# Fourth attention: the next x is turned ahead of the scores, and the query is projected between the turn of the outputs and the values

## The reference

```python
# _layernorm(x) is what comes in as modality1, ctx_768 as modality2
x1 = layernorm(modality1, ln1_g, ln1_b)      # so x is normalized twice
x2 = layernorm(modality2, ln2_g, ln2_b)
q = x1 @ Wq + bq
k = x2 @ Wk + bk
v = x2 @ Wv + bv
scores = jnp.einsum('bqe,bke->bqk', q, k) * scaling
attn = jax.nn.softmax(scores, axis=-1)
ctx = jnp.einsum('bqk,bke->bqe', attn, v)
return ctx @ Wo + bo
```

## Time and profile before

| | |
|---|---|
| median of three runs | 1800.82 us |
| time of the profiled execution | 1798.77 us |
| its span, first to last instruction | 1796.9 us |
| mean granted clock of TensorE | 0.950 |
| PE busy | 1619.2 us (90% of the span) |
| DVE busy | 981.3 us (55%) |
| ACT busy | 624.8 us (35%) |
| POOL busy | 333.5 us (19%) |
| fourth attention, first scores to last projection | 1490.6 to 1646 us |

### The profile page before, as it was taken

One profiled execution on the slowest core, in us unless ns is written; L12 is line 12 of the kernel. 1 busy time (PEld: TensorE's weight loads), 2 busy tenths in 40 slices (PEclk: granted clock), 3 DMA queues, 4 the chain that ended last, 5 costly groups with the idle time before them and its releaser, 6 DMA issues.

```text
span 1796.9 us, 31011 instructions
## 1 busy us (share of the span) xinstructions
PE 1619.2 (90%) x9150; PEld 1153.7 (64%) x9150; DVE 981.3 (55%) x3200; ACT 624.8 (35%) x1772; POOL 333.5 (19%) x465
## 2 busy tenths in 40 slices
PE   6898899859999999999999999799998998887787
PEld 2555555659999866666666667567776446665555
DVE  4778787542222244444444435645555666884764
ACT  3555555412323233333333333133332004552232
POOL 4555555320000130000000000100000122333000
PEclk8999999869999989999999989899998999998887
DMA  4000005248999610000000000100000001310000
GB/s 109 15 18 20 20 19 146 65 138 298 321 327 319 232 41 13 7 12 12 12 12 6 1 4 16 31 26 19 19 25 1 27 25 35 91 56 1 1 19 19
DMA packets 86297, 115.80 MB, mean 64 GB/s; under 512 B 16610, under 2 KB 77762, under 8 KB 81090
## 3 DMA queue, kind: packets, MB, share of 16 engines
q1 hardware_dynamic: 82722, 110.43, 19.1%
q0 software_dynamic: 2432, 4.34, 0.8%
q10 hardware_dynamic: 1056, 0.01, 0.0%
HBM read 104.51 MB, written 6.95 MB: 62 GB/s over the span
## 4 chain that ended last, share of the span: by engine, by line
PE 73%; issue 9%; DVE 7%; ACT 4%; DMA 2%; POOL 2%; ACTq 1%; SPq 0%; DVEq 0%; POOLq 0%
PE bank L2293 14%; PE bank L2406 8%; PE bank L2589 7%; PE bank L2379 5%; PE bank L2682 5%; PE bank L2352 5%; PE bank L2390 4%; PE bank L2436 4%; PE bank L2603 3%; PE bank L2344 3%; PE bank L2635 3%; PE bank L2651 3%; PE bank L2754 2%; DMA work<-in_F_b1c 2%; DVE work L1542 1%
## 5 line engine op out<-in xcount | busy, mean ns | idle before, releaser
L1052 ACT ACTIVATE work<-bank,work 100x361 f32<-100x361 f32 (+1 forms) x272 | 158.9, 591 | 253.5 <-DVE work L1542 231.6
L1551 DVE COPY work<-bank 128x300 f32<-128x300 f32 (+1 forms) x272 | 123.2, 490 | 175.6 <-PE bank L2390 174.9
L2406 PEld LDWEIGHTS bank<-work 128*100 128x100 f32 x1760 | 185.4, 171 | 45.5 <-issue 31.4
L2406 PE MATMUL bank<-work 128*100 128x64 f32 (+1 forms) x1760 | 188.2, 258 | 4.2 <-DVE work L1551 4.2
L2589 PE MATMUL bank<-work 128*128 128x128 f32 x1216 | 144.4, 277 | 3.7 <-DMA work<-in_F_b1c 3.7
L1905 DVE SCALAR_TENSOR_TENSOR work<-bank,work 128x128 f32<-128x128 f32 x160 | 56.1, 351 | 163.8 <-PE bank L2589 151.6
L2589 PEld LDWEIGHTS bank<-work 128*128 128x128 f32 x1216 | 142.0, 193 | 5.3 <-issue 3.5
L1542 DVE TENSOR_REDUCE work<-bank 100x1 f32<-100x361 f32 x208 | 101.8, 528 | 70.9 <-PE bank L2379 65.7
L823 POOL TENSOR_TENSOR work<-work,neg_half 100x1 f32<-100x1 f32 x96 | 52.5, 547 | 391.8 <-DVE work L1498 390.1
L2379 PE MATMUL bank<-work 64*100 64x361 f32 (+1 forms) x512 | 119.0, 542 | 1.1 <-ACT work L1037 0.6
L2293 PE MATMUL bank<-L_WkvT,work 96*128 96x512 f32 x192 | 98.2, 637 | 15.8 <-ACT work L1013 14.9
(11 more groups left out here) (306 smaller groups left out, 2907.9 us busy)
## 6 DMA issues: line engine op xcount, KB each, us to landing
work<-in_F_w SPq DMA_DIRECT2D x58, 1024.0 KB, 5.5
work<-in_ctxT SPq DMA_DIRECT2D x64, 135.4 KB, 2.1
work<-in_ctx SPq DMA_DIRECT2D x32, 192.0 KB, 2.5
work<-in_F_b SPq DMA_DIRECT2D x20, 128.0 KB, 5.8
work<-sorted_x SPq DMA_DIRECT2D x20, 128.0 KB, 2.5
sorted_y<-work SPq DMA_DIRECT2D x20, 128.0 KB, 5.3
work<-in_ctx SPq DMA_DIRECT2D x32, 78.8 KB, 2.4
F_weight<-in_F_w SPq DMA_DIRECT2D x2, 1024.0 KB
```

Source lines behind the costliest of these rows:

```text
L1052: nc.scalar.activation(pr[:, 0:NK], S_bank[k][0:T, 0:NK], ACT.Exp, bias=nmax[k][0:T, :], accum_out=rsum[j][0:T, h:h + 1]).then_inc(s.exped ...
L1551: nc.vector.tensor_copy(PT[k][:, 0:CH, :], PT_bank[k][:, 0:CH * T].rearrange("p (c t) -> p c t", c=CH)).then_inc(s.probs_copied.sem, 1)
L2406: ins = nc.tensor.matmul(to, PT[k][:, c, :], values, start=(c == 0), stop=(c == CH - 1))
```

## The change

Only the order of PE and ACT in the fourth attention changes, with the bank of each step and one wait that follow from it. In `attend(t)` PE now issues `x_turn` of batch t + 1 ahead of `scores` of batch t, and the query projection of batch t + 1 between `o_turn` and `value` of batch t - 1, instead of behind `probs_turn`. ACT copies in the new order. The places of the steps, and so their banks, become 0, 3, 1, 2, 4. No instruction is added or removed; DVE, POOL and the DMA queues keep theirs in the same order.

```diff
@@ -30,12 +30,12 @@
 
 
 PAIRS = (2, 4, 2, 0)
-EARLY = ((0, 1, 5), (0, 1, 2), (0, 1, 2), (0, 1, 2))
+EARLY = ((0, 1, 5), (0, 1, 2), (0, 1, 2), (0, 3, 1, 2))
 GROUPS = (
     ((2, 6, 8, 3), (4, 9, 10, 7)),
     ((3, 4), (5, 6), (7,), (8,)),
     ((3, 4), (5, 6)),
-    ((3, 4),),
+    ((4,),),
 )
 STEPS = tuple(len(e) + sum(len(g) for g in gs) for e, gs in zip(EARLY, GROUPS))
 NORMS = (2, 1, 1, 2)
@@ -65,6 +65,7 @@
 TURN_AT = 256
 BATCHES_BACK = ((0, 2), (2, 6), (6, 11), (11, B))
 KEYS_FIRST = (1, 3, 4, 5, 6, 7, 8, 0, 2)
+QUERY_SECOND = (0, 3, 1, 2, 4)
 SLOTS_AT_ONCE = 4
 SLOT_ROUNDS = B // (2 * SLOTS_AT_ONCE)
 PICK_PARTS = ((0, 4), (4, 8), (8, 12), (12, B))
@@ -149,7 +150,10 @@
 
 def place_of(L, t, n):
 
-    return KEYS_FIRST.index(n) if L == 1 and isinstance(t, int) and t == 0 else n
+    first = isinstance(t, int) and t == 0
+    if L == 3:
+        return n if first else QUERY_SECOND.index(n)
+    return KEYS_FIRST.index(n) if L == 1 and first else n
 
 
 def steps_of(L, t):
@@ -1087,11 +1091,13 @@
                 def attend(t, j, more):
                     started = not (isinstance(t, int) and t == 0)
                     if L == 3:
+                        if more:
+                            step(t + 1, 1 - j, 0)
                         if started:
                             o_copy(t - 1, 1 - j)
+                        exp(t, j, 0)
                         if more:
-                            step(t + 1, 1 - j, 0)
-                        exp(t, j, 0)
+                            step(t + 1, 1 - j, 3)
                         if started:
                             v_copy(t - 1, 1 - j)
                     else:
@@ -1100,7 +1106,7 @@
                         if started:
                             o_copy(t - 1, 1 - j)
                     for n in EARLY[L]:
-                        if more and not (L == 3 and n == 0):
+                        if more and not (L == 3 and n in (0, 3)):
                             step(t + 1, 1 - j, n)
                     if PAIRS[L] == 0:
                         for h in range(H):
@@ -2329,7 +2335,7 @@
                                              start=(c == 0), stop=(c == 1))
                         else:
 
-                            wait_for(pe, s.copied, done + 4)
+                            wait_for(pe, s.copied, done + place_of(3, t, 3) + 1)
                             for c, (lo, m) in enumerate(((0, CW[0]), (HALF, CW[1] + 1))):
                                 for e in range(2):
                                     ins = mm(dst[0:m, c * T:(c + 1) * T], wk3[:, e, lo:lo + m], QT[j][:, e, :],
@@ -2459,15 +2465,17 @@
 
                 def attend(t, j, more):
                     started = not (isinstance(t, int) and t == 0)
+                    if L == 3 and more:
+                        step(t + 1, 1 - j, 0)
                     scores(t, j, 0)
                     if H > 1:
                         scores(t, j, 1)
                     if started:
                         o_turn(t - 1, 1 - j)
                     for n in EARLY[L]:
-                        if more:
+                        if more and not (L == 3 and n == 0):
                             step(t + 1, 1 - j, n)
-                        if L == 3 and n == 0 and started:
+                        if L == 3 and n == 3 and started:
                             value(t - 1, 1 - j)
                     if L == 3 and started:
                         project(t - 1, 1 - j)
```

## The result

The kernel with the change took 1856.87 us, the median of four runs (1844.59 to 1859.3). Beside it the kernel before took 1800.14 us, also in four runs (1793.05 to 1805.83). The ratio is 1.0305 with a 95% interval of 1.0275 to 1.0336, so the change costs about 55 us. The forecast was 1849 us, its range 1812 to 1866, with a chance of 0.80 for slower. The profiled execution of the kernel after took 1856.15 us, with a span of 1854.3 us against 1796.9, and a mean granted clock of 0.93 against 0.95.

The account below looks back on a forecast made before the run. DVE's list, with POOL's small answers, was taken to bound the loop, PE following. +20.5 - 0.4 - 2.6 = +17.5 us at full clock, +30.6 for the clock, gave +48.1 on 1800.8: 1849 us, range 1812 to 1866.

Parts of the forecast that it names:

- The ring through the scores: In the loop, scores queue behind the turn of x, which waits for the second norm; norm to maximum 1.64 us against 0.52.
- The distance from the maximum to the copy: On DVE, from the maximum to the copy of the probabilities: 4.30 us a batch, a cost of 0.48 us.
- part 1: Moving the turn of x of batch t + 1 ahead of the scores of batch t: cost 1.12 us a batch.
- From the copy to the norm: On DVE, from the copy of the probabilities to the end of the second norm: 4.84 us, as before.
- The full-clock period: From one second norm to the next in the loop, at full clock: 10.78 us against 9.20 before.
- The clock: PE idling 3.2 us before each turn of x lowers its clock: 2.35 us a batch, +30.6 us over 13.
- The loop's sum: Over 13 distances between second norms: +20.5 us at full clock, less 0.4 for the first, +30.6 for the clock.
- The start: In the first batch the query fills PE's 2.00 us wait, so weighing and DVE go on 2.6 us earlier.
- The end: From the norm of batch 15 to the scores of batch 15: comes out even, no cost.
- The clock that stays at 1.00: Rival: the ring through the scores forms in the loop but the clock does not fall; 1818 us, chance 0.22.
- The third case: Rival: PE's own ring sets the loop's pace, so not slower; 1789 us, or 1798 if DVE alone does; chance 0.08.
- banks and query add no wait: In the loop's new order, the query fits PE's wait for the outputs' copy, and every step finds a free bank.

Follow-up runs that it names:

- e3: The changed kernel plus ten unneeded matmuls ahead of each turn of x from batch 1 on, in PE's wait for the norm: 1823.58 us, ratio 1.0146.
- e10: The changed kernel with the query back behind the turn of the probabilities, plus seven unneeded matmuls a batch ahead of the turn of x: 1829.64 us, ratio 1.0142.
- e7: The kernel before, with the new order of PE and ACT in the first batch alone: 1796.61 us, ratio 0.9985.
- e4: The changed kernel with DVE reordered in the loop: second norm ahead of the residual, mixture's norm behind the next maximum: 1803.35 us, ratio 1.0032.
- e1: The changed kernel with the query back behind the turn of the probabilities; turn of x stays ahead of the scores: 1840.63 us, ratio 1.0252.
- e2: The changed kernel with the turn of x back behind the scores and the outputs' turn; query stays ahead of the values: 1855.37 us, ratio 1.0330.
- e8: The kernel before, with the new order in the first batch alone and unneeded matmuls in PE's waits in the tail: 1793.69 us, ratio 0.9966.
- e9: The kernel before, PE and ACT in old order, with DVE's second norm ahead of the residual and mixture's norm behind the next maximum: 1846.22 us, ratio 1.0269.

## Why the prediction was right

**The ring through the scores (cost 1.12 us a batch)** was right. In e3 norm to maximum took 1.70 us where 1.64 was worked out.

**The distance from the maximum to the copy (4.30 us)** was right in size: e3 has 4.53 and 4.36. But the prediction's heading put this 0.48 to the query, and e10 shows that it belongs to the turn: with the query in its old place the distance is 4.53 and 4.36 too, and the period is the same. The cause was named correctly in the text (PE's lead, lost by part 1, had hidden the waits for ACT); the query only fits into a wait that is there anyway.

**From the copy to the norm (4.84 us)**: 4.83 in e3. The full-clock period of 10.78 us became 10.95, the missing 0.17 being mostly that of the maximum to the copy.

**The clock (2.35 us a batch)** was right in the mean, and of all the terms it owed most to chance: 13.23 less 10.95 is 2.28. The wait that was to cost the clock is there (3.14 us where 3.2 was worked out), but two things about it were wrong.

It does not cost the clock in every batch. The prediction took the middle of two bounds, 1.5 and 3.2, and few batches lie there: from maximum to maximum 8 of 13 take 13.9 to 14.1 us, which is the upper bound; two in a row took 11.8 and 11.3, and the first 10.6, which is under the lower one. The mean falls between.

And it costs other instructions than those priced. The prediction had the turn and the scores at half clock and the projection back at full. In the batch shown above the turn runs at full clock and the scores only in part at half; query and values are slow as in the upper bound, and so are the turns of the context and most of the projection, which the sum left at full clock:

```profile
1601.25 1.49 PE L2286 MATMUL bank<-ident,work 128*96 128x128 f32 x6
1602.53 1.52 PE L2442 MATMUL bank<-L_Wo,work 128*100 128x256 f32 x4
```

At full clock these take 0.82 and 1.11 us (e3, at 1649.69 and 1650.53). So the size came out in part through errors that cancel.

The Trainium skill, "TensorE: Matmul & The Clock Gate", section "A second HAM failure mode: psum-queue depth-cycling", says of a bf16 kernel that short idling between groups of matmuls can make the clock swing again and again. The fp32 loop here swings too, between 1.00 and 0.50 in the windows above, and the mean of 0.76 against the 1.00 of e3, with the same order of work, agrees with it.

**The loop's sum** over 13 distances: forecast 20.5 - 0.4 + 30.6 = +50.7 us, measured +51.0.

**The start (-2.6 us)**: -3.5, in the kernel after and in e7 alike (8.7 us from the scores of batch 0 to the second norm of batch 2, where it was 12.2). I had counted the earlier weighing alone; it also ran at full clock, 1.22 us where it had taken 2.13. The wait of 2.00 us, said to shrink by about half, became 1.31.

**The end (0)** was the step that was off. From the norm of batch 15 to its scores it took 3.9 us longer. I had counted that stretch at full clock, and it starts with the clock of the loop: the scores of batch 14 took 2.62 us and query and values behind them 1.91 each. In e3, whose clock stays up, the same stretch takes 7.7 us (1645.98 to 1653.68), as before the change. This is the largest part of what the sum missed: the spans differ by 57.4 us where it gave 48.1. Of the other 5.4, 3.0 lie ahead of the changed code and 2.9 behind the scores of batch 15, both no more than runs of one kernel differ among themselves (the four of the kernel after by 14.7 us), and the start gave 0.9 back.

**The rivals.** The clock that stays at 1.00 (1818) is what e3 shows with fillers, 1823.6; without them it did not happen. The third case, PE's own ring as the pace, needed a norm that is ready before the weighing ends; e4 comes nearest to it, and even there PE waits 1.44 us for the norm. What no case of the prediction had is that the query alone costs as much as the whole change. That banks and query add no wait held only because the turn of x had moved up too; by itself the query stands right behind its own x.

**What stays open.** By their ratios e1 lost 45 us and e2 59; why the clock was up for more of e1's loop (0.89) than of e2's (0.74) was not settled. In the traces e1 waits for ACT and for the norm (0.84, 0.67 and 1.03 to 1.46 us a batch), and e2 for DVE and ACT (1.49 and 1.11), and in e4 1.44 and 0.34 leave the clock at 1.00; these are few cases, and no run varied one wait by itself. Nor is it shown why the same wait of 3.14 us costs the clock in most batches of the kernel after and not at 1621.86.

## What to carry to other kernels

In an engine that works in order, an instruction that waits late takes all that stands behind it along: before moving one ahead of a ready group, look whom that group feeds, and whether that engine makes what the moved one waits for. Here this closed a ring, which added 1.7 us to the 9.2 of a batch, and the idle time that it left cost 2.3 more through TensorE's clock. Where PE has to wait in a short stretch, a few matmuls of no use, which together take less time than the wait, can keep the clock up (e8). To bring the awaited result forward on the other engine opens the ring (e4, 9.79 us a batch), but only for the order it was made for, and it did not beat the kernel before: the same edit with PE's old order closed another ring and cost 2.7% (e9).

## What was unexpected of the hardware

Ten unneeded matmuls a batch made the program faster by 33 us (1856.87 to 1823.58), and 14 in the tail, in six groups, took 3.4 us from a stretch of 18.8. Whether waiting costs the clock did not follow its length alone: e4, with 1.44 and 0.34 us of waiting in a batch of 9.8 us, kept 1.00 from 1530 to 1620 us, while the kernel before fell to 0.50 in its tail after waits of 0.84 and 0.67 us, with PE busy for 1.89 of 3.40 us. And in the loop of the kernel after the clock mostly fell only when PE had ended its wait, 0.8 to 1.7 us behind the start of the turn of x, so that the work behind it paid the price.
